# Attention over 8,192 context rows on one core: one PSUM bank moved from scores to maxima, a sixth slot for exponentials, and three steps moved

## The chip, the cores and the metric

The kernel runs on one core of one Trainium2 chip. The metric is the device time of one execution in microseconds (us), as the median of several runs. The engines are called PE (TensorE), DVE (VectorE), ACT (ScalarE), POOL (GpSimd) and SP (SyncE, which only issues transfers here).

## The reference, cut to what matters

Two batches of 512 tokens (x, 512 wide) go through three residual blocks: attention to a context of 8,192 rows of 384 numbers, then a Mamba-like block with an MLP, then a quantised feed-forward block. The change touches the first of them, and the edges of the second by the PSUM banks:

```
x = x + xattn(layernorm(x), ctx_768, ...)
x = x + attn(layernorm(x), ...)
x = x + ffn(layernorm(x), ...)

def xattn(x, y, ...):                       # 16 heads of 32
    q = (x @ Wq + bq); k = (y @ Wk + bk); v = (y @ Wv + bv)
    scores = einsum('bnhd,bmhd->bhnm', q, k) / sqrt(32)
    out = einsum('bhnm,bmhd->bnhd', softmax(scores), v)
    return relu(out @ W1 + b1) @ W2 + b2
```

## The kernel before, in words

**Tiling.** The context is worked in 16 chunks of 1,024 rows (8 for each batch). A chunk has four groups of four heads, so there are 64 groups. I call a chunk's groups first to fourth. A group has 32 units: 8 tiles of 128 context rows by 4 heads. `UPG` is 32, `NGT` is 64, `HG` is 4, `MT` is 8. I number the scores of a group 0 to 31. The loop's step i of line 1942 issues score i + 2, so the code's "step 16 of a group" is where score 18 is issued, step 24 belongs to score 26, and step 29 to score 31.

**Two passes over the keys.** The softmax is done in running form. A first pass (`fill("A")`, line 1828) multiplies queries by keys into a work bank, and DVE takes the maximum of each 128x512 tile (`empty`, line 1052). When a group's 32 maxima are there, `new_max` (lines 1078 and 1080) forms the new running maximum `mn` and its negative `nm`; PE transposes it (line 1832, the item "M"), DVE splits it into `Th` and `Tl`, and SP writes it as extra rows beside the queries. The second pass (`scores`, line 1854) multiplies again, with the maxima subtracted, into one of the score banks; ACT takes the exponential of each 128x512 score into `pf` (`probabilities`, line 1536). The first pass runs 41 units ahead: just before score 23 of a group stands the first fill of the group after next, which waits for that group's keys (`keys_stacked`, line 1826).

**Keys and values.** `fill_side` (lines 1805 and 1812) computes them in pieces between the scores, from the context as two rounded parts, `cTh` (rounded, ACT, line 1493) and `cTl` (the remainder, POOL, line 863). Keys come in halves K0 and K1, values as V0 and V1, all in bank 7. The second half of the keys, K1, is begun just behind score 3. When it is done, ACT and DVE copy it out (KH, KL), and SP issues twelve transfers that stack it into `ks` (`stack_keys`, line 656).

**Weighted values and sums.** Every eighth step PE multiplies two tiles of `pf` by the values (`burst`, `values`, line 1867, rows `x16` in the trace). `pf` has `P_SLOTS` = 5 slots of one tile (4 heads) each. For the denominators POOL adds the tiles 0 to 6 of a group into `psum` (six additions of 128x2048, line 899); tile 7 is added by an accumulating transfer that POOL issues (line 905). Then PE sums over the partitions (`sums`, line 1884) at burst `SUM_BURST`. A slot is free for ACT when PE has used it and POOL has added it; for tile 7's slot that means when the transfer has landed. With five slots this wait stands ahead of the exponential of score 16 of the next group.

**POOL's other duties in a group:** after the third addition `keep_max` (line 873), which waits for DVE's `mn`; behind the transfer `rescale` (line 855); and in the second group of a chunk both halves of the next chunk's `cTl`, the first half ahead of the first addition, the second ahead of the sixth (`LOW_AT`). ACT computes the scaling factor `al` of the next group (`shrink`, line 1507) at step 24.

**PSUM.** Eight banks of 128x512: work banks 0 and 1 (`WORK_BANKS`; maxima and the transposes M, T and D take turns there), score banks 2, 3 and 4, the denominators in 5, the outputs in 6, keys and values in 7. A fill waits until DVE has emptied the tile `WORK_BANKS` before it; a score waits for the exponential `S_BANKS` before it:

```
pe.wait_ge(s_wfree, work_count(x))            # fill, line 1819
if u >= S_BANKS:                              # scores, line 1850
    pe.wait_ge(s_exp, (u - S_BANKS + 1))
```

**The lead-in** (lines 1919 to 1941) turns the normalised x of both batches, computes q in banks 2 to 5, and the first keys, values and maxima. All order is written out by hand in each engine's block.

Of the kernel before, what the change touches and what calls it, by code (L numbers as in the profile page):

```python
# [30 lines left out]
MT = CH // P  # L31
# [28 lines left out]
NGT = NB * NGB  # L60
UPG = HG * MT
UNITS = NGT * UPG
A_UNITS = NT * BLK
A_AHEAD = UPG + 9
WORK_BANKS = 2
S_BANK = 2
S_BANKS = 3
DEN_BANK = 5
O_BANK = 6
SIDE_BANK = 7  # L70
# [19 lines left out]


LOW_GROUP = 1
LOW_AT = {0: 0, 5: 1}
P_SLOTS = 5
BURST = 2
BURSTS = NGT * MT // BURST
ADDS = MT - 2
KEEP_ADD = 3
LAST_SUMMED = 4
LAST_ADDS = LAST_SUMMED - 1  # L100
SUM_BURST = MT // BURST + 1
STEPS = (NGT - 1) * UPG + T_LAG + D_LAG + 1
ATTENDED = UNITS - UPG + T_LAG - UPG + 2
TURNED = UNITS + BURST * HG + 2
# [30 lines left out]
def work_at(i):  # L135

    u, items = i + SB_AHEAD, []
    if u + A_AHEAD < NGT * HG * A_UNITS:
        items.append(("A", u + A_AHEAD))
    if u % UPG == M_STEP and u // UPG + 1 < NGT:  # L140
        items.append(("M", u // UPG + 1))
    g, r = divmod(i - T_LAG, UPG)
    if 0 <= g < NGT and r == 0:
        items.append(("T", g))
    if 0 <= g < NGT and r == D_LAG and g % NG == NG - 1:
        items.append(("D", g // NG))
    return items
# [16 lines left out]
def high_at(i):  # L164

    u = i + SB_AHEAD
    c, half = u // (NG * UPG) + 1, HIGH_AT.get(u % (NG * UPG))
    return [(c, half, f) for f in range(KC)] if half is not None and c < NB * NCH else []


def low_at(g, n):

    c = g // NG + 1
    if g % NG == LOW_GROUP and n in LOW_AT and c < NB * NCH:
        return c, LOW_AT[n]
    return None
# [4 lines left out]
WORK_POS, SIDE_POS = {}, {}  # L181
# [3 lines left out]
    if _x not in SIDE_POS:  # L185
        SIDE_POS[_x] = len(SIDE_POS)
WORK_N, SIDE_N = len(WORK_POS), len(SIDE_POS)
assert WORK_N % WORK_BANKS == 0


def side_bank(x):
# [5 lines left out]
def side_ends(i):  # L197

    part = side_at(i)
    return part[0] if part and last_piece(*part) else None  # L200
# [44 lines left out]
def stage(b, name):  # L245

    n = {"ln_q_T": NT, "q": KD, "att_T": NT, "xw1": F1 // P, "xw2": NT, "rms_T": NT, "xz": 2 * KD, "dbc": 1,
         "dt": KD, "conv": KD, "ssm": KD, "mix_out": NT, "ln2_T": NT, "ffn1": F2 // P, "ffn2": NT, "ln3_T": NT, "lora1": 1,
         "fc": F2 // P, "lora2": 1, "proj": NT}[name]
    return [(b, name, i) for i in range(n)]  # L250
# [2 lines left out]
ALL_BANKS = tuple(range(8))  # L253
LOW, HIGH = ALL_BANKS[:4], ALL_BANKS[4:]
SEGMENTS = [
    ((2, 3, 4, 5), stage(0, "ln_q_T") + stage(0, "q") + stage(1, "ln_q_T") + stage(1, "q")),
    ((7, 2, 3, 4), stage(0, "att_T") + stage(0, "xw1")),
    (ALL_BANKS, stage(1, "att_T") + stage(0, "xw2")
     + stage(1, "xw1")[:AHEAD_1] + stage(0, "rms_T") + stage(0, "xz")[:6] + stage(0, "dbc") + stage(0, "dt")
     + stage(0, "xz")[6:] + stage(1, "xw1")[AHEAD_1:]),  # L260
# [21 lines left out]
def emit(nc, t_in, out):  # L282
    with ExitStack() as ctx:
# [3 lines left out]
        def sb(name, shape, dt=F32, c=ctx):  # L287
            return c.enter_context(nc.sbuf_tensor(name, shape, dt))
# [96 lines left out]
        ps = ctx.enter_context(nc.psum_tensor("ps", [P, 8, 512], F32))  # L385
# [59 lines left out]

        pf = sb("pf", [P, P_SLOTS, HG * NTOK], c=att)
        psum = sb("psum", [P, 2, HG * NTOK], c=att)
# [11 lines left out]
        def place(name, at, shape, dt=F32):  # L459

            with ExitStack() as c:
                if at:
                    sb("below_" + name, [P, at], mybir.dt.uint8, c)
                return sb(name, shape, dt, c)
# [19 lines left out]
        xw1 = place("xw1", 96 * K, [P, 2, KD, F1 // 2])  # L484
# [95 lines left out]
        def work_count(x):  # L580

            return WORK_POS[x] + 1

        def work_bank(x):

            return ps[:, WORK_POS[x] % WORK_BANKS, :]

        def side_count(x):

# [20 lines left out]
        def _(sp):  # L610
# [33 lines left out]
            def save_out(b):  # L644

                sp.wait_ge(s_wfree, work_count(("D", b * NCH + NCH - 1)) + WORK_BANKS)
                sp.dma_start(o_rows[b], Oacc[:]).then_inc(s_osave, 16)
# [11 lines left out]
            def max_rows(g):  # L659

                sp.wait_ge(s_wfree, work_count(("M", g)) + WORK_BANKS)
                for r, src in enumerate((Th, Tl)):
# [168 lines left out]
        def _(pool):  # L831
# [15 lines left out]
            def rescale(of):  # L847

                pool.wait_ge(s_alpha, of + 1)
                if of >= NG:  # L850
                    pool.wait_ge(s_wfree, work_count(("D", of // NG - 1)) + WORK_BANKS)
                if of // NG == NCH:
# [35 lines left out]
            for g in range(NGT):  # L888
# [4 lines left out]
                for n in range(adds):  # L893
# [3 lines left out]
                    pool.wait_ge(s_exp, HG * (tile + 1))  # L897
                    before = pf[:, (tile - 1) % P_SLOTS, :] if n == 0 else acc
                    pool.tensor_tensor(acc, before, pf[:, tile % P_SLOTS, :], ALU.add).then_inc(s_sum, 1)  # L899
                    pool.wait_ge(s_sum, g * ADDS + (n + 1))  # L900
                    if n == KEEP_ADD - 1 and g + 1 < NGT:
                        keep_max(g + 1)
                if g < NGT - 1:
                    pool.wait_ge(s_exp, HG * (g + 1) * MT)
                    pool.dma_start(acc, pf[:, (g * MT + MT - 1) % P_SLOTS, :], accum_op=ALU.add
                                   ).then_inc(s_tail, 16)
# [11 lines left out]
        def _(dve):  # L918

            dve.memset(cols[:, COL["eps"][0]:COL["eps"][0] + 1], EPS).then_inc(s_eps, 1)  # L920
            for i in range(8):
                dve.memset(stats[0][:, 0, 0:1], 0.0).then_inc(s_free[i], 1)
                dve.wait_ge(s_free[i], 1)
            dve.memset(stats[0][:, 0, 0:1], 0.0).then_inc(s_wfree, WORK_BANKS)
            dve.wait_ge(s_wfree, WORK_BANKS)
# [546 lines left out]
        def _(act):  # L1472
# [16 lines left out]
            def high_context(c, i, f):  # L1489

                part = slice(i * CH // 2, (i + 1) * CH // 2)
                act.wait_ge(s_ctx[i], 16 * (c + 1))
                act.copy(cTh[:, f, part], cT[:, f, part]).then_inc(s_chi[i], 1)
# [8 lines left out]
            def shrink(of):  # L1502

                act.wait_ge(s_dm, of + 1)
                if of > 1:
                    act.wait_ge(s_resc, of - 1)
                act.activation(al[:, of % 2, :], dm[:], ACT.Exp, scale=SCALE).then_inc(s_alpha, 1)

            def take_side(x):

                act.wait_ge(s_side, side_count(x))
                src = ps[:, side_bank(x), :]
                if x[0] == "K":
                    if x[1] > 0:
                        keys_stacked(act, x[1] - 1)
                    act.activation(KH[:, x[2] * 512:(x[2] + 1) * 512], src, ACT.Identity,
                                   bias=col("bk", x[1] % NG)).then_inc(s_kvh, 1)
                else:
                    pair, q = x[1] // 2, x[1] % 2 * 2 + x[2]
                    if q == 0 and pair >= 2:  # L1520
                        act.wait_ge(s_pv, MT * (2 * pair - 2))
                    act.copy(V[:, pair % 2, q * VM:(q + 1) * VM, :].rearrange("p m d -> p (m d)"), src  # L1522
                             ).then_inc(s_vfree, 1)

            def probabilities(u):

                act.wait_ge(s_sb, (u + 1))
                tile, j = divmod(u, HG)
                if j == 0 and tile >= P_SLOTS:
                    of, r = divmod(tile - P_SLOTS, MT)  # L1530
                    act.wait_ge(s_pv, of * MT + (r + 1))
                    if r < MT - 1:
                        act.wait_ge(s_sum, of * ADDS + max(r, 1))
                    else:
                        act.wait_ge(s_tail, 16 * (of + 1))
                act.activation(pf[:, tile % P_SLOTS, j * NTOK:(j + 1) * NTOK], ps[:, S_BANK + u % S_BANKS, :],  # L1536
                               ACT.Exp, scale=SCALE).then_inc(s_exp, 1)
# [32 lines left out]
            for i in range(STEPS):  # L1570
                side = side_ends(i - 1)
                if side and side[0] == "K":
                    take_side(side)
                if i + SB_AHEAD < UNITS:
                    probabilities(i + SB_AHEAD)
                if side and side[0] == "V":
                    take_side(side)
                for part in high_at(i):
                    high_context(*part)
                if i % UPG == 1 and 1 <= i // UPG <= NGT:  # L1580
                    take_out(i // UPG - 1)
                if i % (NG * UPG) == BURST * HG * (SUM_BURST - MT // BURST + 1) + 1 and i // (NG * UPG) > 0:
                    take_sums(i // (NG * UPG) - 1)
                for x in work_at(i):
                    if x[0] == "M":
                        shrink(x[1])
            arrive(act)

            def hidden(b, fs):
# [135 lines left out]
            for j in range(PAIRS):  # L1725
                b, i = divmod(j, S_ALL)
                q, e = divmod(i, KD)
# [30 lines left out]
        def _(pe):  # L1758
# [84 lines left out]
            def scores(u):  # L1843
# [4 lines left out]
                if n == 0:  # L1848
                    pe.wait_ge(s_mrow[g % NG], (g // NG + 1) * 32)
                if u >= S_BANKS:  # L1850
                    pe.wait_ge(s_exp, (u - S_BANKS + 1))
                if u == UPG * (KS - 1):
                    pe.wait_ge(s_ones2, 16)
                pe.matmul(ps[:, S_BANK + u % S_BANKS, :], ks[0:SROWS, keys_of(g, j), m * P:(m + 1) * P],  # L1854
                          qs[0:SROWS, h, :], start=True, stop=True).then_inc(s_sb, 1)
# [42 lines left out]
            def burst(n):  # L1898

                if n < BURSTS:  # L1900
                    for tile in range(BURST * n, BURST * (n + 1)):
                        values(tile)
                g, rest = divmod(n - SUM_BURST, MT // BURST)
                if g >= 0 and rest == 0:
# [319 lines left out]
```

## Time and profile before

| what | us |
|---|---|
| median of 3 runs | 3052.53 (3051.62 to 3055.20) |
| profiled execution | 3053.57 |
| its span, first to last instruction | 3051.7 |
| busy PE / DVE / POOL / ACT | 2932.7 / 2237.6 / 2021.2 / 1676.0 |
| mean granted TensorE clock | 0.990 |

The lead-in lasts until score 0 at 87.67 us, the loop over groups until about 2260 us, and the rest of the program to the end. Matmuls overlap one another in the trace (a 512-column one shows as 0.40 us, but the next starts 0.23 us later), so the starts are to be read, not the sum of the durations. In a row of the timeline the bracket at the end gives the idle time before the row, and whose work ended it.

### The profile page before, as it was taken

To read this page: it belongs to the slowest core of one execution; us is meant where nothing else is said; L and a number is where in the kernel's file an instruction comes from. 1 tells how busy PE (TensorE), PEld (TensorE's weight loads), DVE (VectorE), ACT (ScalarE), POOL (GpSimd) and SP (SyncE) were. 2 spreads that over 40 slices of the span, in tenths; PEclk is the share of its full clock that TensorE was granted. 3 is DMA by queue.
4 is the path that set the end of the run, shared out by engine and by line. 5 is a ranking of instruction groups with operands and counts; after the bars stand their busy time and mean duration, and the time that the engine had idled before them with its cause. 6 is when DMAs were issued, how large, how long until landed. Compare 5 with 4: busy or idle time off the path is not lost. (4 is left out here: it accounts for less than half of the span.)

```text
span 3051.7 us, 39907 instructions
## 1 busy us (share of the span) xinstructions
PE 2932.7 (96%) x14712; PEld 1802.4 (59%) x14712; DVE 2237.6 (73%) x3368; ACT 1676.0 (55%) x2920; POOL 2021.2 (66%) x745
## 2 busy tenths in 40 slices
PE   7999999999999999999999999999999877899999
PEld 4666666666666666666666666666534333344477
DVE  7777777777777777777777777777746899986653
ACT  1566666666666666666666666666641555321021
POOL 1699998999999998999999899999950000000000
PEclk9999999999999999999999999999999999999999
DMA  6534543454435455453444444443450112214200
GB/s 166 136 81 101 114 107 91 96 116 100 101 84 115 102 122 126 104 121 87 101 95 118 95 95 104 114 104 81 87 178 25 47 63 97 79 59 167 69 14 18
DMA packets 108886, 296.10 MB, mean 97 GB/s; under 512 B 23762, under 2 KB 28882, under 8 KB 99122
## 3 DMA queue, kind: packets, MB, share of 16 engines
q1 hardware_dynamic: 99044, 226.71, 26.8%
q0 software_dynamic: 9072, 66.06, 11.8%
q8 instruction: 117, 1.92, 0.3%
q10 hardware_dynamic: 576, 0.79, 0.1%
q14 instruction: 77, 0.63, 0.1%
HBM read 114.46 MB, written 8.06 MB: 40 GB/s over the span
## 5 line engine op out<-in xcount | busy, mean ns | idle before, releaser
L1052 DVE TENSOR_REDUCE pm<-ps 128x1 f32<-128x512 f32 x2048 | 1407.8, 691 | 542.3 <-PE ps L1828 472.2
L1536 ACT ACTIVATE pf<-ps 128x512 f32<-128x512 f32 x2048 | 1212.4, 599 | 707.9 <-PE ps L1854 562.6
L899 POOL TENSOR_TENSOR psum<-psum,pf 128x2048 f32<-128x2048 f32 x317 | 1455.9, 4593 | 25.1 <-ACT pf L1536 8.9
L1828 PE MATMUL ps<-ks,qs 96*128 96x512 f32 x2048 | 847.5, 414 | 21.0 <-DVE pm L1052 12.5
L1854 PE MATMUL ps<-qs,ks 98*128 98x512 f32 x2048 | 813.8, 398 | 2.3 <-ACT pf L1536 2.2
L1828 PEld LDWEIGHTS ps<-ks,qs 96*128 96x128 f32 x2048 | 387.0, 189 | 284.9 <-issue 155.8
L1867 PE MATMUL ps<-pf,V 128*32 128x512 f32 x4096 | 492.7, 598 | 0.0
L1854 PEld LDWEIGHTS ps<-qs,ks 98*128 98x128 f32 x2048 | 391.0, 191 | 50.1 <-ACT pf L1536 13.8
L914 POOL PARTITION_ALL_REDUCE qstat<-qstat x2 | 0.7, 365 | 603.2 <-DVE qstat L1350 603.2
L899 POOL TENSOR_TENSOR psum<-pf 128x2048 f32<-128x2048 f32 x64 | 303.1, 4735 | 37.0 <-ACT pf L1536 36.9
L1805 PE MATMUL ps<-cTh,Wkg 128*128 128x512 f32 x732 | 293.2, 401 | 13.4 <-POOL cTl L863 10.2
L1867 PEld LDWEIGHTS ps<-pf,V 128*32 128x32 f32 x4096 | 106.7, 109 | 244.0 <-issue 197.8
L1812 PE MATMUL ps<-Wvh,cTh 128*128 128x256 f32 x768 | 224.3, 292 | 0.0
L1812 PE MATMUL ps<-Wvl,cTh 128*128 128x256 f32 x768 | 219.0, 285 | 0.0
L1812 PE MATMUL ps<-Wvh,cTl 128*128 128x256 f32 x768 | 218.0, 284 | 0.0
L2057 PE MATMUL ps<-bx,ident 128*128 128x512 f32 x256 | 134.7, 655 | 54.1 <-DVE bx L1320 54.1
L1805 PEld LDWEIGHTS ps<-cTh,Wkg 128*128 128x128 f32 x732 | 139.0, 190 | 60.8 <-ACT V L1522 30.1
L1812 PEld LDWEIGHTS ps<-Wvl,cTh 128*128 128x128 f32 x768 | 146.5, 191 | 27.2 <-issue 1.5
L1812 PEld LDWEIGHTS ps<-Wvh,cTh 128*128 128x128 f32 x768 | 146.1, 190 | 25.9 <-issue 1.2
L1812 PEld LDWEIGHTS ps<-Wvh,cTl 128*128 128x128 f32 x768 | 145.9, 190 | 22.5 <-issue 1.0
L1314 DVE TENSOR_TENSOR_SCAN bx<-dA,bx 128x512 f32<-128x512 f32 x128 | 149.3, 1208 | 1.5 <-ACT dA L1734 1.4
L1805 PE MATMUL ps<-cTl,Wkg 128*128 128x512 f32 x366 | 144.8, 396 | 0.0
(224 smaller groups left out, 3016.0 us busy)
## 6 DMA issues: line engine op xcount, KB each, us to landing
ks<-KH SPq DMA_DIRECT2D x512, 128.0 KB, 3.5
psum<-pf POOLq DMA_DIRECT2D x63, 1024.0 KB, 8.0
ks<-KL SPq DMA_DIRECT2D x256, 128.0 KB, 3.5
cT<-in_ctxT SPq DMA_DIRECT2D x32, 768.0 KB, 4.7
Wkg<-wk_rows SPq DMA_DIRECT2D x61, 384.0 KB, 5.8
BC<-bc_rows SPq DMA_DIRECT2D x32, 512.0 KB, 4.8
ring<-in_ffn_w SPq DMA_DIRECT2D x16, 1024.0 KB, 7.9
wA<-in_W_fcT SPq DMA_DIRECT2D x4, 1024.0 KB, 10.3
```

The costliest lines, as they stand in the source:

```text
L899: pool.tensor_tensor(acc, before, pf[:, tile % P_SLOTS, :], ALU.add).then_inc(s_sum, 1)
L914: pool.partition_all_reduce(qstat[:, i, 1:2], qstat[:, i, 0:1], P, bass.bass_isa.ReduceOp.max).then_inc(s_allmax, 1)
L1052: dve.tensor_reduce(pm[:, n // BLK, n % BLK:n % BLK + 1], src, AX.X, ALU.max).then_inc(s_wfree, 1)
L1314: last = dve.tensor_tensor_scan(bx[:, slot, s, :], dA[:, slot, s, :], bx[:, slot, s, :], 0.0, ALU.mult, ALU.add)
L1536: act.activation(pf[:, tile % P_SLOTS, j * NTOK:(j + 1) * NTOK], ps[:, S_BANK + u % S_BANKS, :], ACT.Exp, scale=SCALE).then_inc(s_exp, 1)
L1805: last = pe.matmul(dst, w[term == 2], (cTh, cTl)[term == 1][:, f, half], start=(n == 0), stop=(n == TERMS - 1))
L1812: last = pe.matmul(dst[:, m * 2 * P:(m + 1) * 2 * P], (cTh, cTl)[term == 2][:, f, t * P:(t + 1) * P], (Wvh, Wvl)[term == 1][:, f, pair], s ...
L1828: last = pe.matmul(dst, qs[0:3 * HD, h, t * P:(t + 1) * P], ks[0:3 * HD, keys_of(of, j), i * 512:(i + 1) * 512], start=True, stop=True)
L1854: pe.matmul(ps[:, S_BANK + u % S_BANKS, :], ks[0:SROWS, keys_of(g, j), m * P:(m + 1) * P], qs[0:SROWS, h, :], start=True, stop=True).then_ ...
L1867: last = pe.matmul(ps[j * HD:(j + 1) * HD, O_BANK, :], V[:, g // 2 % 2, m, at:at + HD], pf[:, tile % P_SLOTS, j * NTOK:(j + 1) * NTOK], st ...
L2057: last = pe.matmul(bank(w), ident[:], bx[:, j % S_SLOTS, s, :], start=(q == 0 and s == 0), stop=(q == S_PER - 1 and s == S_STEP - 1))
```

## The change: what it does

- Work banks: 0, 1 and 4 (three). Score banks: 2 and 3 (two). Bank 4 is taken out of the turns for the lead-in's transposes and queries (now 2, 3, 5) and for the first transposes and products behind the loop (now 7, 2, 3).
- `P_SLOTS` 6: the wait for the transfer of tile 7 stands ahead of the exponential of score 20.
- `SUM_BURST` one later: the sums are issued at step 24, behind score 26, no longer at step 16, behind score 18. ACT's copy of a chunk's denominators (`take_sums`) moves with it.
- `LOW_AT`: the second half of `cTl` ahead of the fifth addition.
- `SHRINK_STEP`: ACT's `al` at step 29.
- The scratch space in SBUF for the transfers that POOL issues: 512 for 2048.

```diff
-WORK_BANKS = 2
+WORK_AT = (0, 1, 4)
+WORK_BANKS = len(WORK_AT)
 S_BANK = 2
-S_BANKS = 3
+S_BANKS = 2
...
-LOW_AT = {0: 0, 5: 1}
-P_SLOTS = 5
+LOW_AT = {0: 0, 4: 1}
+P_SLOTS = 6
...
-SUM_BURST = MT // BURST + 1
+SUM_BURST = MT // BURST + 2
+SHRINK_STEP = UPG - 3
...
-    ((2, 3, 4, 5), stage(0, "ln_q_T") + stage(0, "q") + stage(1, "ln_q_T") + stage(1, "q")),
-    ((7, 2, 3, 4), stage(0, "att_T") + stage(0, "xw1")),
+    ((2, 3, 5), stage(0, "ln_q_T") + stage(0, "q") + stage(1, "ln_q_T") + stage(1, "q")),
+    ((7, 2, 3), stage(0, "att_T") + stage(0, "xw1")),
...
-            return ps[:, WORK_POS[x] % WORK_BANKS, :]
+            return ps[:, WORK_AT[WORK_POS[x] % WORK_BANKS], :]
...
-                for x in work_at(i):
-                    if x[0] == "M":
-                        shrink(x[1])
+                if i % UPG == SHRINK_STEP and i // UPG + 1 < NGT:
+                    shrink(i // UPG + 1)
...
-    nc = _bacc.Bacc("TRN2", target_bir_lowering=False, num_devices=1, dynamic_dma_scratch_size=2048)
+    nc = _bacc.Bacc("TRN2", target_bir_lowering=False, num_devices=1, dynamic_dma_scratch_size=512)
```

**PE around the sums.** On PE, in every group, before, from the scores 17 and 18 to the next pieces of keys:

```order
L1854 MATMUL ps<-qs,ks 128x512
L1867 MATMUL ps<-pf,V 32x512 x8
L1884 MATMUL ps<-psum,sel 32x512 x4
L1828 MATMUL ps<-ks,qs 128x512
L1854 MATMUL ps<-qs,ks 128x512
L1805 MATMUL ps<-cTh,Wkg 128x512
```

and with the change, in the same group, first the same place and then (behind the line of dots) that of scores 25 to 27:

```order
L1854 MATMUL ps<-qs,ks 128x512
L1867 MATMUL ps<-pf,V 32x512 x8
L1828 MATMUL ps<-ks,qs 128x512
L1854 MATMUL ps<-qs,ks 128x512
L1805 MATMUL ps<-cTh,Wkg 128x512
...
L1832 MATMUL ps<-ident,nm 16x128
L1867 MATMUL ps<-pf,V 32x512 x8
L1884 MATMUL ps<-psum,sel 32x512 x4
L1828 MATMUL ps<-ks,qs 128x512
L1854 MATMUL ps<-qs,ks 128x512
```

The four matmuls of the sums (L1884) leave the place between score 18 and fill and score 19, and stand eight scores later, behind the transposed maxima (L1832) and the next burst.

**POOL in the second group of a chunk,** before, from the copies of `keep_max` to the transfer:

```order
L884 COPY pm<-m_run 128x16
L899 TENSOR_TENSOR psum<-psum,pf 128x2048 x2
L863 TENSOR_TENSOR cTl<-cT,cTh 128x3x512
L899 TENSOR_TENSOR psum<-psum,pf 128x2048
L905 DMA psum<-pf 128x2048
```

and with the change (its lines are one further down):

```order
L885 COPY pm<-m_run 128x16
L900 TENSOR_TENSOR psum<-psum,pf 128x2048
L864 TENSOR_TENSOR cTl<-cT,cTh 128x3x512
L900 TENSOR_TENSOR psum<-psum,pf 128x2048 x2
L906 DMA psum<-pf 128x2048
```

One addition passes behind the remainder; the transfer stays last.

## Rows read from the trace of the kernel before

**Rows 1.** Who waited for whom, 600 to 2300 us: total, times, longest.
```profile
PE ps L1828 <- DVE pm L1052: 8.2, 17, 1.9
PE ps L1805 <- POOL cTl L863: 7.4, 11, 0.7
```
**Rows 2.** Timeline of PE and DVE, second groups: start, duration, engine, line, what.
```profile
695.04 0.50 PE L1828 MATMUL ps<-ks,qs 96*128 96x512 f32 x1 [0.30 <-DVE pm L1052]
...
1240.64 0.50 PE L1828 MATMUL ps<-ks,qs 96*128 96x512 f32 x1 [1.90 <-DVE pm L1052]
...
693.63 0.76 DVE L1080 TENSOR_SCALAR nm<-mn 128x16 f32<-128x16 f32 x1
```
**Rows 3.** Timeline of PE and POOL, K1 in a third and a first group.
```profile
571.52 0.47 PE L1805 MATMUL ps<-cTh,Wkg 128*128 128x512 f32 x1 [0.67 <-POOL cTl L863]
...
775.08 0.40 PE L1854 MATMUL ps<-qs,ks 98*128 98x512 f32 x1
775.57 0.51 PE L1805 MATMUL ps<-cTh,Wkg 128*128 128x512 f32 x1
...
567.91 3.46 POOL L863 TENSOR_TENSOR cTl<-cT,cTh 128x1536 fp32r<-128x1536 f32 x1
```
**Rows 4.** Timeline of PE, same third group: sums, next fill, and the awaited fill.
```profile
587.21 1.04 PE L1884 MATMUL ps<-psum,sel 128*32 128x512 f32 x8
588.18 0.50 PE L1828 MATMUL ps<-ks,qs 96*128 96x512 f32 x1
...
592.92 0.47 PE L1828 MATMUL ps<-ks,qs 96*128 96x512 f32 x1 [1.20 <-issue]
```
**Rows 5.** Timeline of SP and PE: a stack of keys, third group and then first.
```profile
578.32 0.53 SPq L656 DMA_DIRECT2D ks<-KH  x1
...
646.60 0.53 SPq L656 DMA_DIRECT2D ks<-KH  x1
...
654.98 0.59 SPq L656 DMA_DIRECT2D ks<-KH  x1
...
659.63 0.39 PE L1828 MATMUL ps<-ks,qs 96*128 96x512 f32 x1
```
**Rows 6.** Timeline of POOL and ACT around the third group's start.
```profile
576.24 0.88 POOL L905 DMA_DIRECT2D psum<-pf  x1 [0.30 <-DVE pm L1052]
...
560.85 1.67 ACT L1493 CAST cTh<-cT 128x512 fp32r<-128x512 f32 x3
...
586.76 1.57 ACT L1536 ACTIVATE pf<-ps 128x512 f32<-128x512 f32 x3 [3.42 <-DMA psum<-pf]
```
**Rows 7.** The page, DMA issues: KB each, median us to landing.
```profile
ks<-KH SPq DMA_DIRECT2D x512, 128.0 KB, 3.5
psum<-pf POOLq DMA_DIRECT2D x63, 1024.0 KB, 8.0
```
**Rows 8.** Timeline of ACT and PE: exponentials of scores 4 to 6, then score 6.
```profile
743.26 1.75 ACT L1536 ACTIVATE pf<-ps 128x512 f32<-128x512 f32 x3
...
743.98 0.40 PE L1854 MATMUL ps<-qs,ks 98*128 98x512 f32 x1
```
**Rows 9.** Timeline of PE, POOL and DVE, end of the loop over groups.
```profile
2254.97 1.04 PE L1884 MATMUL ps<-psum,sel 128*32 128x512 f32 x8
...
2192.22 0.22 POOL L873 TENSOR_TENSOR dm<-m_run,mn 128x16 f32<-128x16 f32 x1 [2.01 <-issue]
...
2244.02 9.90 POOL L899 TENSOR_TENSOR psum<-psum,pf 128x2048 f32<-128x2048 f32 x2
...
2260.14 2.87 DVE L983 COPY tT<-ps 128x512 f32<-128x512 f32 x4 [1.53 <-PE ps L1768]
```
**Rows 10.** Timeline of PE and DVE in the lead-in.
```profile
18.13 0.77 PE L1805 MATMUL ps<-cTh,Wkh 128*128 128x512 f32 x1 [1.55 <-DVE cTl L1018]
...
78.50 0.49 PE L1828 MATMUL ps<-ks,qs 96*128 96x512 f32 x1 [1.05 <-DVE pm L1052]
...
19.10 2.86 DVE L983 COPY xqT<-ps 128x512 f32<-128x512 f32 x4
```

More of the change, by code:

```diff
@@ L187 @@
 WORK_N, SIDE_N = len(WORK_POS), len(SIDE_POS)
-assert WORK_N % WORK_BANKS == 0
 def side_bank(x):
```

## The prediction

> **What bounds the kernel now.** I read the page first: PE is busy 96% of the span, and its few idle stretches are what a change like this can win. In the waits of PE inside the loop over groups [rows 1] two causes stand out, 17 waits for DVE's maxima and 11 for POOL's remainder `cTl`. As a matmul shows as 0.40 us but the next starts 0.23 us later, a matmul with idle time g before it is late by g + 0.17. So [rows 1] come to 8.2 + 17 x 0.17 = 11.1 us and 7.4 + 11 x 0.17 = 9.3 us in 1,660 us. Next I placed each wait in its group by the timeline, and it is always the same three places in a chunk of four groups (some 136 us):
>
> - Second group, fill before score 25: late by 0.47 us, once by 2.07 [rows 2]. DVE has just reduced the last maximum of a group and formed `mn` and `nm`, and with two work banks PE can't run ahead of it. Sixteen groups have it, 12 of them inside [rows 1] with 7.3 us of the 11.1; all sixteen come to 9.8 us.
> - Third group, first key matmul of K1: late by 0.84 us, since the second half of `cTl` ends at 571.4 [rows 3]. Fifteen groups.
> - Third group, fill before score 23: late by 1.37 us in this chunk [rows 4]. Its releaser is shown as "issue", once and again as DVE; what it really waits for are the twelve transfers of the new keys. In this third group the fill starts 592.92 - 578.32 = 14.60 us after the first of them was issued; in a first group 659.63 - 646.60 = 13.03 us, without idle, and there the last transfer was issued at 654.98, so that it landed before 659.63 by the page's 3.5 us [rows 5, 7]. In the third group POOL's 1 MB transfer was issued at 576.24, 2.1 us before the keys' first [rows 6], and both share the DMA engines. I looked at all fifteen: 13.6 to 14.8 us, mean 14.1.
>
> ACT waits too, 3.42 us for the landing of POOL's transfer ahead of the exponential of score 16 [rows 6]. In PE that is only a late copy of V0 behind score 18, 0 to 0.6 us, which in turn shortens the wait before score 23: the keys decide.
>
> **The change part by part.**
>
> 1. *Third work bank.* The fill before score 25 now needs the maximum three before it. DVE needs 0.69 us for one and a step of PE is 0.70 us, so the bank forgives 0.7 us: the usual 0.47 goes, of the 2.07 some 1.4 stays, of one of 1.12 another 0.4. Each late matmul also costs 0.1 us behind it. 9.8 + 1.6 - 1.8 - 0.2: **-9.4 us**. Bounds: 0 (if DVE is late for another reason each time) and -11.4.
>
> 2. *Second half of `cTl` one addition earlier.* It would end 4.6 us sooner, at 566.8. Its input `cTh` is written by ACT until 562.5 [rows 6], 0.6 us before the fourth addition ends, so POOL doesn't wait. Then K1 waits for the copy of V0, as it does in a first group: 775.57 - 775.08 - 0.23 = 0.26 us [rows 3]. Gain 0.84 - 0.26 = 0.58, 15 times: **-8.7 us**. Bounds: 0 and -12.6.
>
> 3. *Sums behind score 26.* They take 588.18 - 587.21 = 0.97 us of PE [rows 4], of which I take 0.9 (a burst straight before a fill has a tail too). PE's total is the same, but they leave the stretch between the keys' first transfer and the fill before score 23. Where that stretch is set by the transfers, PE now waits 0.9 us longer, and the sums come on top behind it. Fifteen third groups: **+13.5 us**. In the other groups PE needs 13.03 - 0.9 = 12.1 us there and the keys were in time by 0.7 to 3.3 us; only the tightest is then late: **+0.3 us**. Bounds: 0 (the keys land sooner by as much) and +14.6. Waits of the sums for the transfer, 0.04 to 0.5 us in some third groups, are already inside.
>
> 4. *Sixth slot.* ACT's wait moves to score 20. In third groups the transfer landed 2.8 us ahead of score 20; the sums' move and items 1 and 2 take 2 us of that, so ACT hardly waits. The copy of V0 is in time, but its gain goes into the wait before score 23: **0**. If that cover were gone, it would be -2.7 us.
>
> 5. *Two score banks.* A score now waits for the exponential two before it. The tightest place is score 6: in [rows 8] three exponentials run from 743.26 in 1.75 us, so the first (score 4) ends at 743.86, and score 6 starts at 743.98: 0.12 us of room, where 0.06 is needed. Other steps have 0.37 or more; the only negative ones stand behind ACT's wait for the transfer, which item 4 takes away. **0**. Bounds: nothing, and one late ACT copy (0.58 us, 0.26 more than the 0.37 of room less 0.06) in each of 62 groups, +16.
>
> 6. *`al` at step 29.* 0.24 us of ACT beside steps with 0.5 us of room: **0**. The smaller scratch: POOL's issue takes 0.88 us [rows 6] and a transfer is over before the next is issued, 34 us later: **0**.
>
> 7. *End of the loop.* The last sums wait for POOL, whose chain has no gap from its last wait for DVE at 2192.2 (2.01 us long) to the end of its additions at 2253.92 [rows 9]. DVE's `mn` there comes 0.9 us sooner, as the sums have moved behind it, so POOL ends at 2253.0, and the sums can start there rather than at 2254.97, because ACT is no longer held up from score 16 on. The transposes and DVE's copies, at 2260.14, follow: **-1.8 us**. The three banks for them cost nothing: the fourth transpose waits for a copy of 0.7 us that DVE makes anyway.
>
> 8. *Lead-in.* The fourth transpose of x now waits for DVE's first copy, which ends at 19.8; before, the keys could start at 18.13 [rows 10]. They start at about 20.8, run through both halves, and the second half, bound by DVE's `cTl` before, ends 1.3 us later: +1.3. The maxima's waits (1.22 us at 78.50 [rows 10], 0.7 behind it, a few of 0.1 to 0.4) shrink: -2.3. **-1.0 us**; bounds +2.3 and -2.3.
>
> Sum: -9.4 - 8.7 + 13.5 + 0.3 - 1.8 - 1.0 = **-7.1 us** against the profiled execution's own 3053.6, so 3046.5; the median of the runs lies 1.0 below that one, so **3045.5 us**.
>
> **A rule against a row.** POOL's 1 MB transfers take 8.0 us in the median [rows 7], and item 3 rests on that: the transfer is under way for most of the keys' stack. The Trainium skill ("DMA: Bandwidth & Descriptors", Anatomy of one DMA — SWDGE (gpsimd) path) fits such a transfer as 2.0 us plus its bytes over 436 GB/s, an estimate of 4.4 us here, over soon after the keys begin. By it the keys would land as in other groups and rival A holds; this trace disagrees (7.0 at least).
>
> **Rivals.**
>
> - *A: the keys aren't the gate, or land sooner.* Then item 3 costs nothing and item 4 gains: 3045.5 - 13.5 - 2.7 = 3029. For it: the trace names DVE for some of these waits. Against: third groups take 13.6 us or more each time, with or without the late V0.
> - *B, the other side: two score banks.* If any of ACT's copies runs one place later than now, PE waits at once: at score 6, or where the room is 0.37. Price +16 (item 5): 3062. It decides from 0.06 us at score 6. Against: ACT's order hardly moves.
> - *C: the gains come short.* `nm` took 0.76 us in [rows 2] while POOL was adding. An addition takes 4.6 us; if `nm` meets it earlier, DVE is late by more than a bank forgives, and item 1 shrinks to -3; with a lead-in at +2.3: 3045.5 + 6.4 + 3.3 = 3055. The Trainium skill ("SBUF — State Buffer", Who interferes with whom) has it as a lock held for a whole instruction, which the 2.07 us fits. Against: in second groups DVE and POOL both move by 0.9 us, so they meet as before.
> - *D: the smaller scratch* makes POOL wait for its own transfer: some 7 us a group on an engine with about 1.6 us to spare, +300 us. Nothing in the trace speaks for it.
>
> **How the numbers follow.** Forecast 0.50, A 0.14, B 0.11, C 0.24, D 0.01. A measurement tells about 0.2%, 6.1 us. The forecast's own spread is 4 us around 3045.5, so six in ten of it lie below 3046.4: faster 0.31 + 0.14 = 0.45 and a little of C, 0.46. Slower (above 3058.6): B, D and a little of C, 0.13. The same: 0.41. The range takes in A's and C's values and half of what leads to B: 3028 to 3058. Both signs are likely, so the forecast's own range: 3041 to 3050.
>
> **What would show it.** Right: no wait before score 25 in second groups; K1's start in third groups 0.26 us late, by V0; in third groups the fill before score 23 still 14 us behind the keys' first transfer, and PE's wait there about 2.0 us instead of 1.0; sums without waits; end of the loop near 2253. Wrong: that wait unchanged or gone (A), scores that wait for exponentials (B), `nm` above 1.5 us or fills that still wait (C).

## The result, and the profile after

The changed kernel takes 3067.16 us (median of 6 runs, 3063.45 to 3079.47) against 3053.32 us before (6 runs, 3051.62 to 3055.20): ratio 1.0055, 95% interval [1.0043, 1.0068]. The forecast was 3045.5 with a range from 3028 to 3058. The kernel became slower by 0.55%, beyond the noise, and the prediction was wrong in sign.

| what | before | after |
|---|---|---|
| profiled execution | 3053.57 | 3068.36 |
| score 32 starts (lead-in over) | 123.94 | 125.17 |
| score 32 to score 1984 | 2075.85 | 2078.22 |
| score 1984 to 2047 (last two groups) | 52.82 | 64.20 |
| from there to the end | 801.0 | 800.8 |
| mean granted TensorE clock | 0.990 | 0.984 |

The starts are those of the rows of L1854. Of the 14.8 us between the two executions 11.4 lie in the last two groups, 2.4 in the 61 before them, 1.2 in the lead-in, and the rest is 0.2 shorter.

**The waits of PE in the loop,** after, 600 to 2300 us (waited for, total, times, longest), answer to [rows 1]:

```profile
PE ps L1828 <- issue: 17.4, 11, 2.2
PE ps L1854 <- ACT pf L1537: 4.6, 16, 0.5
PE ps L1828 <- DVE pm L1053: 1.6, 2, 0.9
PE ps L1832 <- DVE nm L1081: 1.1, 1, 1.1
```

The 17 waits for DVE have become 2, the 11 for `cTl` are gone. Two kinds have grown. The 11 waits of 17.4 us are those of the awaited fill of third groups, where the same 11 groups had 6.3 us before. The 16 waits of scores for exponentials (5 before, 1.4 us) all stand behind 2209 us, in the last two groups: up to 2200 us neither profile shows one.

**A second group,** after, timeline of POOL, DVE and PE around score 25 [rows 2]. `nm` takes 0.76 us as before, and the fills at 694.83 and 695.53 have no idle time before them:

```profile
690.73 4.60 POOL L900 TENSOR_TENSOR psum<-psum,pf 128x2048 f32<-128x2048 f32 x1
...
694.60 0.76 DVE L1081 TENSOR_SCALAR nm<-mn 128x16 f32<-128x16 f32 x1
694.60 0.40 PE L1805 MATMUL ps<-cTh,Wkg 128*128 128x512 f32 x1
...
694.83 0.40 PE L1828 MATMUL ps<-ks,qs 96*128 96x512 f32 x1
695.07 0.40 PE L1854 MATMUL ps<-qs,ks 98*128 98x512 f32 x1
...
695.53 0.40 PE L1828 MATMUL ps<-ks,qs 96*128 96x512 f32 x1
```

**The third group of rows 3 to 6,** after, timeline of PE, POOL and SP:

```profile
563.06 3.51 POOL L864 TENSOR_TENSOR cTl<-cT,cTh 128x1536 fp32r<-128x1536 f32 x1
...
570.50 0.40 PE L1854 MATMUL ps<-qs,ks 98*128 98x512 f32 x1
...
570.99 0.50 PE L1805 MATMUL ps<-cTh,Wkg 128*128 128x512 f32 x1
...
576.17 0.90 POOL L906 DMA_DIRECT2D psum<-pf  x1 [0.37 <-DVE pm L1053]
...
577.80 0.53 SPq L657 DMA_DIRECT2D ks<-KH  x1
...
589.63 0.59 SPq L657 DMA_DIRECT2D ks<-KH  x1
...
592.12 0.48 PE L1828 MATMUL ps<-ks,qs 96*128 96x512 f32 x1 [1.99 <-issue]
592.43 0.50 PE L1854 MATMUL ps<-qs,ks 98*128 98x512 f32 x1
...
593.16 0.63 PE L1828 MATMUL ps<-ks,qs 96*128 96x512 f32 x1
593.58 0.63 PE L1854 MATMUL ps<-qs,ks 98*128 98x512 f32 x1
```

K1 is late by 0.26 us, as forecast. But POOL issues its transfer at 576.17, where before it was 576.24 [rows 6]. The group starts at the same time as before (566.29 and 566.25) and PE has gained some 1.6 us in it, 0.6 at K1 and 1.0 by the moved sums; half of that shows in the fill, which comes at 592.12 for 592.92, and half has become wait, 1.99 us for 1.20. The fill does wait for the keys: by the trace's landing times the last of the twelve, issued at 589.63, lands at 592.03, and the fill starts 0.09 us later. The same 0.09 us stands behind each of the 94 such fills with idle time above 0.2 us in the seven kernels below where they wait. POOL's transfer has landed by then, at 585.66. Behind the fill the matmuls stand 0.42 us apart and show as 0.63: the granted clock has fallen from 2.4 to 1.2 GHz. Two such stretches, windows of after (PE, PEld, DVE, ACT, POOL busy, then the granted clock, DMA share, GB/s):

```profile
592.20:596.00 3.80, 3.80 (x10) 2.96 (x11) 2.08 (x3) 1.66 (x3) 3.74 (x4) 0.55 0.00 0
...
1278.30:1282.30 4.00, 3.96 (x11) 3.12 (x12) 2.19 (x4) 1.63 (x3) 3.86 (x5) 0.57 0.01 2
```

A fall lasts 3.41 us here; there are five in the loop, all straight behind this fill where it was 1.87 to 2.41 us late. Before there was none, and this fill was late by 1.54 us at most.

**The last two groups,** windows of before and then of after, the same columns:

```profile
2215.00:2230.00 15.00, 14.52 (x83) 5.44 (x80) 5.64 (x11) 9.40 (x19) 14.70 (x6) 1.00 0.26 89
2230.00:2245.00 15.00, 11.64 (x68) 4.24 (x60) 4.91 (x4) 7.50 (x15) 14.54 (x6) 1.00 0.92 284
```

```profile
2215.00:2230.00 15.00, 13.54 (x66) 5.55 (x68) 10.65 (x17) 8.52 (x16) 14.70 (x6) 0.92 0.14 28
2230.00:2245.00 15.00, 13.11 (x44) 3.90 (x36) 0.00 (x0) 8.59 (x17) 13.46 (x6) 0.73 0.90 317
2245.00:2260.00 15.00, 13.40 (x53) 4.63 (x53) 6.76 (x5) 9.20 (x17) 13.74 (x4) 0.84 0.26 53
```

PE does 44 instructions where it did 68, at a granted clock of 0.73 where it had 1.00. The timeline there, of before and then of after:

```profile
2225.57 4.03 ACT L1536 ACTIVATE pf<-ps 128x512 f32<-128x512 f32 x8 [1.53 <-PE ps L1854]
2226.22 2.46 PE L1854 MATMUL ps<-qs,ks 98*128 98x512 f32 x5 [0.22 <-ACT pf L1536]
2228.61 1.92 PE L1867 MATMUL ps<-pf,V 128*32 128x512 f32 x16
2230.47 0.96 PE L1854 MATMUL ps<-qs,ks 98*128 98x512 f32 x3
2231.00 0.60 ACT L1536 ACTIVATE pf<-ps 128x512 f32<-128x512 f32 x1 [1.40 <-PE ps L1854]
```

```profile
2217.40 9.20 POOL L900 TENSOR_TENSOR psum<-psum,pf 128x2048 f32<-128x2048 f32 x2
...
2223.56 0.98 PE L1854 MATMUL ps<-qs,ks 98*128 98x512 f32 x2 [0.21 <-ACT pf L1537]
...
2224.24 2.40 DVE L1081 TENSOR_SCALAR nm<-mn 128x16 f32<-128x16 f32 x1
...
2226.78 0.27 PE L1832 MATMUL ps<-ident,nm 128*16 128x128 f32 x1 [1.05 <-DVE nm L1081]
...
2226.98 3.13 PE L1867 MATMUL ps<-pf,V 128*32 128x512 f32 x16
...
2229.86 1.60 PE L1884 MATMUL ps<-psum,sel 128*32 128x512 f32 x8
2231.39 0.73 PE L1854 MATMUL ps<-qs,ks 98*128 98x512 f32 x2
2231.92 2.97 ACT L1537 ACTIVATE pf<-ps 128x512 f32<-128x512 f32 x5 [5.56 <-PE ps L1854]
```

Behind the last fill PE has only scores, values, sums and a few transposes. Scores go two at a time where they went three to five at a time, a burst takes 3.13 us at the lower clock for 1.92, and ACT, with at most two scores in stock, stands idle for 5.56 us beside late `nm`, the burst and the sums.

### The profile page after: what moved, and what is told of

The parts are those of the page before. It is cut to its first block, busy times and chain, and to the rows that moved or that the text cites. A ratio compares the mean times of both kernels' runs of the same rounds, so it can differ in the third digit from the quotient of the medians.

```text
span 3066.6 us, 39906 instructions
## 1 busy us (share of the span) xinstructions
PE 2946.3 (96%) x14712; PEld 1814.0 (59%) x14712; DVE 2250.4 (73%) x3368; ACT 1685.1 (55%) x2920; POOL 2022.5 (66%) x745
## 3 DMA queue, kind: packets, MB, share of 16 engines
q8 instruction: 117, 1.92, 0.3%
## 4 chain that ended last, share of the span: by engine, by line
PE 89%; DVE 7%; ACT 2%; issue 2%; DMA 0%; SPq 0%; ACTq 0%; DVEq 0%
PE ps L1828 16%; PE ps L1867 16%; PE ps L1854 15%; PE ps L1781 9%; PE ps L1812 9%; PE ps L1805 8%; PE ps L2077 4%; PE ps L2041 4%; PE ps L2057 2%; PE ps L1884 2%; DVE pm L1053 2%; DVE bx L1315 1%; PE ps L1836 1%; PE ps L2069 1%; ACT V L1523 1%
## 5 line engine op out<-in xcount | busy, mean ns | idle before, releaser
L1854 PE MATMUL ps<-qs,ks 98*128 98x512 f32 x2048 | 824.0, 403 | 6.8 <-ACT pf L1537 6.5
L1854 PEld LDWEIGHTS ps<-qs,ks 98*128 98x128 f32 x2048 | 393.1, 192 | 75.9 <-ACT pf L1537 31.9
```

## The experiments

Three theories were put up after this reading. Theory 1, mine: the moved sums lengthen the wait of third groups, and the clock falls behind it. Theory 2: all of the loss is the two score banks. Theory 3: the sums' move costs nothing. Theory 4 came out of the first four runs.

**Undoing parts.** sums_back:

```diff
-SUM_BURST = MT // BURST + 2
+SUM_BURST = MT // BURST + 1
```

> The changed kernel with the sums at step 16 again, behind score 18; all else as changed. Theory 1 (the moved sums make PE wait 1.9 us and more ahead of score 23 in some third groups, the granted clock falls to 0.5 for 3.4 us after it, and the two score banks cost only at the end of the loop): that wait goes back to about 1.0 us, no fall of the clock between 101 and 2200 us, 3.4 us less by score 1984 for each of the chunks at 137.7 us or more (five, some 9 us) and 13 us for the waits themselves: 3067 - 22 = 3045 us, the last two groups still some 10 us too long. Theory 2 (all of the loss is in the two score banks): the waits go, but only by what they are, 13 us: 3054 us or more, and the chunks keep falls of the clock. Theory 3 (moving the sums costs nothing, the keys land with them): 3065 to 3069.

Measured 3062.33 us (ratio 1.0041 [1.0029, 1.0053]): 5 us better by the medians, 3.4 us against the kernel before beside each, and not 22. The intervals of the two ratios overlap, and the loop of the profile is no shorter (2079.05 us, 2078.22 with the sums moved). The third groups are as long (the table below), and the clock still falls. So the sums don't carry the loss as theory 1 had it, and theory 3's figure was nearest.

banks_back undoes the banks:

```diff
-WORK_AT = (0, 1, 4)
+WORK_AT = (0, 1)
...
-S_BANKS = 2
+S_BANKS = 3
...
-    ((2, 3, 5), stage(0, "ln_q_T")
+    ((2, 3, 4, 5), stage(0, "ln_q_T")
...
-    ((7, 2, 3), stage(0, "att_T")
+    ((7, 2, 3, 4), stage(0, "att_T")
```

> The changed kernel with two work banks and three score banks again, and the lead-in and the first stages behind the loop on their old banks; all else as changed. Theory 1: the 10 us of groups 62 and 63 and some 2 us ahead of score 6 come back, the fills ahead of score 25 are late again (9.4 us), and the falls of the clock in third groups stay: 3067 - 12 - 1 + 9 = 3063. Theory 2 (the score banks are all of the loss, 24 us against the forecast): 3067 - 24 + 9 = 3052. In both, score 2047 stands less than 26 us behind score 2016 (before 25.3, changed 33.3).

Measured 3048.61 us (0.9990 [0.9982, 0.9999]), better than either theory had it, and less than before, with the sums moved. So the banks carry the whole loss and more; the 51.8 us of the last two groups bear out that part.

sums_banks_back is both edits together; low_only is the kernel before with `LOW_AT = {0: 0, 4: 1}`.

> The changed kernel with both taken back: what is left is the sixth slot, the second half of cTl ahead of the fifth addition, al at step 29 and the small scratch. Theory 1: the forecast's item 2 alone, -8.7 us, and up to -2.7 more where the copy of V0 is no longer held up: 3042 to 3045 us, and no fall of the clock in the loop. A rival (the small scratch or the sixth slot costs something of its own): above 3048.

> The kernel before with only the second half of cTl ahead of the fifth addition. By item 2 of the prediction -8.7 us: 3044.5 us, K1 in third groups late by 0.26 us. If instead the gain only goes into the wait ahead of score 23, which the keys' landing sets after K1's own start: since the keys are issued sooner by as much, it should not; a result above 3049 would speak for that.

Measured 3047.68 us (0.9983 [0.9974, 0.9992]) and 3047.95 us (0.9988 [0.9979, 0.9996]). The sixth slot, the small scratch and `al` together cost and bring nothing in the medians (0.8 us in the loops of the profiles). Between these runs the sums' move costs 0.9 us (3048.61 against 3047.68; 3.1 us in the loop of the profiles, 2068.53 and 2071.66), where the forecast had 13.8. With three work banks the median shows 4.8 (sums_back), without a trace of it in the loop.

**What gates the third group.** The table puts the profiles side by side: mean time from score 0 of second and third groups to the next group's, then in third groups the issue of POOL's transfer and the awaited fill, both behind score 0, and the time at half clock and for the last two groups (starts of rows; the means are over 15 groups).

| kernel | 2nd group | 3rd group | transfer | fill | half clock, loop | last two groups |
|---|---|---|---|---|---|---|
| before | 34.28 | 35.23 | 10.02 | 26.18 | 0 | 52.8 |
| low_only | 34.37 | 34.58 | 9.99 | 25.50 | 3.4 | 53.6 |
| sums_banks_back | 34.53 | 34.47 | 9.94 | 25.30 | 6.8 | 54.9 |
| banks_back | 34.66 | 34.56 | 9.05 | 24.59 | 6.8 | 51.8 |
| after | 33.79 | 35.87 | 9.88 | 25.43 | 17.1 | 64.2 |
| sums_back | 33.69 | 35.99 | 10.70 | 26.72 | 10.2 | 64.3 |
| short_add | 33.80 | 33.54 | 5.60 | 23.69 | 0 | 61.7 |
| tile7_pe | 33.80 | 34.40 | none | 24.55 | 0 | 62.4 |
| late_banks | 33.80 | 36.29 | 9.89 | 25.56 | 27.3 | 54.5 |
| tile7_late | 33.80 | 34.40 | none | 24.55 | 0 | 53.5 |
| tile7_banks_back | 34.77 | 34.38 | none | 24.54 | 10.2 | 52.5 |
| tile7_late_sums_back | 33.69 | 34.39 | none | 25.41 | 0 | 55.1 |

In the seven kernels where the fill waits, it stands in the mean 15.4 to 16.2 us behind POOL's issue, but 13.1 to 15.2 us behind the first issue of the keys. Moving the sums makes POOL's issue come 0.9 us sooner behind score 0 (9.94 to 9.05), and the third work bank makes it come 0.8 us later (9.05 to 9.88), since the second group is shorter and POOL's chain is not: counted from score 0 of the second group (the first two columns added, second group and transfer) POOL's issue comes at 43.71 us in banks_back and 43.67 in after. The awaited fill, counted so, comes at 59.25 and 59.22: what the bank gains in the second group, 0.87 us, is gone at that fill. In banks_back no third group has a fall of the clock behind it (its 6.8 us stand in second groups), with fills late by 1.43 us at most.

That is theory 4: POOL's transfer and the keys share the DMA engines (from 576 to 593 us in after the keys' queue takes 49.2% of the 16 engines and POOL's 31.1%), and the pair is over a fixed time behind POOL's issue. The fixed time is one of means; single fills stand 14.7 to 17.3 us behind POOL's issue, and what sets the rest isn't shown. Two runs change the transfer itself, one by leaving it out, one by issuing it sooner. tile7_pe (`tail_by_pe(g)` is true for second groups, and the second piece stands in `values`; the changed waits of ACT and of the sums are left out here):

```diff
-                    pool.wait_ge(s_exp, HG * (g + 1) * MT)
-                    pool.dma_start(acc, pf[:, (g * MT + MT - 1) % P_SLOTS, :], accum_op=ALU.add
-                                   ).then_inc(s_tail, 16)
+                    if not tail_by_pe(g):
+                        pool.wait_ge(s_exp, HG * (g + 1) * MT)
+                        pool.dma_start(acc, pf[:, (g * MT + MT - 1) % P_SLOTS, :], accum_op=ALU.add
+                                       ).then_inc(s_tail, 16)
...
+                if m == MT - 1 and tail_by_pe(g):
+                    for j in range(HG):
+                        pe.matmul(ps[j * HD:(j + 1) * HD, DEN_BANK, :], sel[:, g % NG, :],
+                                  pf[:, tile % P_SLOTS, j * NTOK:(j + 1) * NTOK], start=False, stop=False)
```

> The changed kernel, but in second groups POOL issues no transfer: tile 7 of the group is summed by PE, four matmuls ahead of its values. Theory 4 (formed from the first four runs: in every group of every kernel the keys land 15.2 to 16.5 us behind the issue of POOL's transfer, so in third groups it is POOL's transfer, issued 9.9 us behind score 0, that sets the fill ahead of score 23, not the issue of the keys): without it the keys land in time as far as 12 us behind their issue suffice; the wait of 1.7 us and the falls of the clock behind it (0.4 us a group in the mean) go, PE pays 0.9 us for the four matmuls: 15 x (0.9 - 2.2) = -20 us: 3047 us. Theory 1 (the keys take 13.8 us from their own issue on): the wait stays, and with the four matmuls at most 0.9 us of it are covered: 3067 or more.

Measured 3041.54 us (0.9963 [0.9950, 0.9975]), some 5 us under theory 4's figure.

short_add leaves most of one tile out of the denominators of each second group, so its result is not the reference's and its time serves only to test the theory:

```diff
+                    cut = slice(0, 64 if g % NG == LOW_GROUP and n == ADDS - 1 else HG * NTOK)
-                    pool.tensor_tensor(acc, before, pf[:, tile % P_SLOTS, :], ALU.add).then_inc(s_sum, 1)
+                    pool.tensor_tensor(acc[:, cut], before[:, cut], pf[:, tile % P_SLOTS, cut], ALU.add).then_inc(s_sum, 1)
```

> The changed kernel, but POOL's sixth addition of each second group takes in only 64 of 2048 columns: most of that tile is left out of the sums, and POOL issues the transfer 4.5 us sooner. Theory 4: the keys land with it, the wait ahead of score 23 in third groups goes, and the clock's falls: 3067 - 33 = 3034 us. Theory 1: 3065 us, the wait unchanged.

Measured 3028.02 us (0.9919 [0.9906, 0.9932]). Its timeline in the same group, SP and PE:

```profile
564.03 0.89 POOL L907 DMA_DIRECT2D psum<-pf  x1 [0.37 <-POOL psum L901]
...
569.97 0.52 SPq L657 DMA_DIRECT2D ks<-KH  x1
...
577.20 1.32 SPq L657 DMA_DIRECT2D ks<-KH  x1
...
582.14 0.40 PE L1829 MATMUL ps<-ks,qs 96*128 96x512 f32 x1
```

The fill is 12.17 us behind the keys' first transfer and doesn't wait; SP issues the twelve in 8.5 us (569.97 to 578.52), where beside the late transfer it needed 12.4 (577.80 to 590.22 in after's timeline, its last issue at 589.63 lasting 0.59). In both runs no third group waits, and the clock doesn't fall once between score 32 and score 1984. Theory 1's gate, the keys' own 13.8 us, has fallen: it asked for 3067 or more and for 3065 us. In the kernels without the transfer in second groups the keys of third groups land 9.8 to 9.9 us behind their first issue in the mean, and beside it 13.0 to 15.0 us: so POOL's transfer is what makes them late.

**The end of the loop.** late_banks gives bank 4 back to the scores behind the last fill (the changed waits that go with it are left out here):

```diff
+LATE_U = UNITS - A_AHEAD + 1
+LATE_W = WORK_POS[("A", UNITS - 1)] // len(WORK_AT) * len(WORK_AT)
+def score_bank(u):
+    return S_BANK + (u % S_BANKS if u < LATE_U else (2, 0, 1)[(u - LATE_U) % 3])
...
-            return ps[:, WORK_AT[WORK_POS[x] % WORK_BANKS], :]
+            n = WORK_POS[x]
+            return ps[:, WORK_AT[n % WORK_BANKS if n < LATE_W else (n - LATE_W) % 2], :]
```

> The changed kernel with bank 4 given back to the scores from score 24 of group 62 on, behind the last fill: three score banks and two work banks from there. If the 11 to 12 us lost in groups 62 and 63 are the two score banks: from score 1984 to score 2047 52 to 54 us in place of 64, and 3055 us. If they are DVE's late nm in group 62 (2.4 us) with the clock's falls behind it: 60 us or more, and above 3062.

Measured 3060.51 us (1.0024 [1.0013, 1.0035]; 3049.10 to 3067.16 in 12 runs). The last two groups take 54.5 us for 64.2, as the first reading had it: the two score banks, and not `nm`, which takes 2.33 us there still. Its timeline there:

```profile
2236.65 0.97 PE L1864 MATMUL ps<-qs,ks 98*128 98x512 f32 x3
2237.19 2.56 ACT L1545 ACTIVATE pf<-ps 128x512 f32<-128x512 f32 x5 [5.79 <-PE ps L1864]
2237.84 2.46 PE L1864 MATMUL ps<-qs,ks 98*128 98x512 f32 x5 [0.22 <-ACT pf L1545]
...
2240.23 1.92 PE L1877 MATMUL ps<-pf,V 128*32 128x512 f32 x16
```

Runs of three to five scores are back, and the burst behind them takes 1.92 us. The median came 5 us short of its forecast; the profiled execution of this kernel had 27.3 us at half clock in the loop, ten more than after's, and was itself one of the slowest of the twelve (3066.55).

**A better version, and the parts in it.** tile7_late is tile7_pe and late_banks together; tile7_banks_back is tile7_pe on the old banks; tile7_late_sums_back is tile7_late with the sums at step 16.

> Both of these edits. Theory 4 and the score banks at the end: 3067 - 20 - 12 = 3035 us, which would beat the kernel before by 0.5%. Theory 1: 3055 us.

> The kernel without the transfer in second groups, but with two work banks and three score banks as before. What the third work bank is worth once POOL's transfer no longer gates the third group. Theory 4 (two gates one behind the other: with the transfer in place what the bank gains in the second group is lost again in the third): the waits ahead of score 25 in second groups stay (0.75 us, 15 times), those of third groups are gone, and the end of the loop is as before: 3037 + 11 - 2 (score 6) = 3046 us. If the bank is worth nothing even then: 3037 us or less.

> The best kernel so far (no transfer in second groups, bank 4 given back at the end) with the sums at step 16 again. Theory 4: with no transfer in the third group the place of the sums doesn't matter there; in the other groups the keys are in time with either (1.6 to 2.4 us of room): 3037 us, within 3. If the sums' place has a cost of its own: the kernel differs by 5 us or more.

Measured 3037.31 us (0.9947 [0.9936, 0.9959]), 3047.28 us (0.9985 [0.9976, 0.9994]) and 3033.03 us (0.9936 [0.9923, 0.9949]). The third work bank, worth less than nothing in the change, is worth 10 us once POOL's transfer doesn't gate the third group (3047.28 to 3037.31, and 14.3 us between score 32 and 1984 of the profiles, where tile7_banks_back has 10.2 us at half clock and the other none). The last is the fastest that computes the whole reference, 18.5 us below the 3051.56 of before beside it. The old place of the sums is 4.3 us better there by the medians, 3.2 against the kernel before beside each, where I had given 3 for the same; 1.6 us of it show in the loop of the profiles, the rest I can't place.

## Why the prediction was wrong, point by point

**Which steps failed.** In the profiles the sum was -7.1 us and became +14.8. Two terms made the kernel slower. Item 5 put the two score banks at 0; in the last two groups, where no fill stands between the scores, they cost some 10 us of the +11.4 that stand where item 7 had -1.8. Item 1 priced the third work bank at -9.4; in the loop it cost 6.6, because what it gained came back as a wait on the awaited fill. These errors are of 13 and 16 us. Item 3, with +13.8 for 3.1 in the loop, erred by 10.7 us the other way and hid part of them, which was luck. The same step failed in items 1 and 3: the landing of the keys was counted from their own first issue, with POOL's transfer as a fixed part of it.

- **Item 1, third bank, -9.4.** Right as far as the second group goes: it went from 34.66 to 33.79 us between banks_back and after, 0.87 us in the mean. The sum over the loop was wrong. The next gate, POOL's transfer, hangs on POOL's chain, and that doesn't shorten with PE's second group: third groups went from 34.56 to 35.87, 0.83 us by the transfer's later issue, the rest mostly by the clock. From score 32 to 1984 the bank costs 6.6 us (2071.66 to 2078.22), though the awaited fill comes no later: some 2 us are score 6, and 17.1 us at half clock for 6.8 make an estimate of 5 us, half of the difference. Rival C's sign did appear: `nm` takes 1.4 to 2.0 us in the fifteen third groups of after. But it begins while PE waits for the keys, and from 600 to 2200 us PE shows no wait for `nm`; in second groups it was long twice, 2.22 and 3.24 us.
- **Item 2, `cTl`, -8.7.** Right in the loop: 8.1 us in the loop of low_only (2075.85 to 2067.77); its median shows 4.0 of them, ratio 0.9988.
- **Item 3, sums, +13.5 and +0.3.** "What it really waits for are the twelve transfers of the new keys" was right: the fill starts 0.09 us behind the last landing. Wrong was what sets that landing, 14 us counted from the keys' own issue. The row of the shared engines was cited beside it [rows 6], but taken as a fixed part of the keys' time, and not as what moves. The mean from POOL's issue is as constant, and the move of the sums pulls that issue forward by 0.9 us. It costs 0.9 us in the medians, 3.1 in the loop. Rival A had "or land sooner", and with it the side on which this item erred, but not what lands them sooner. The Trainium skill's fit of such a transfer ("DMA: Bandwidth & Descriptors", Anatomy of one DMA — SWDGE (gpsimd) path), an estimate of 4.4 us here, is as far off as before: the profile of after has 7.8 us in the median.
- **Items 4 and 6, 0.** Right together: sums_banks_back against low_only, 3047.68 and 3047.95; so rival D is out.
- **Item 5, two score banks, 0.** Wrong twice. Score 6 of second and fourth groups is late by 0.07 us, some 2 us in all, where I had seen 0.12 us of room and a need of 0.06. And the check of the steps ended where fills end: the last 41 scores have no fill between them. Rival B had the side and the part of the machine right, and the place wrong.
- **Item 7, end of the loop, -1.8.** It became +11.4, some 10 of it from the cause just named (9.7 came back in late_banks). I had followed POOL and DVE there, and never asked what paces PE when it has only scores.
- **Item 8, lead-in, -1.0.** It was +1.2, but the seven profiles with this same lead-in have score 32 between 122.00 and 125.17: no verdict.
- **The clock** had no term. A PE wait was priced by its length; behind the longest ones in third groups come 3.41 us at 1.2 GHz. At scores 23 to 25 of third groups this makes 0.42 us in the mean of after, some 6 us in all, and in the last two groups 20.5 us stand at that clock.

How the 10 us of the end divide between waits and clock isn't settled: four profiles with two score banks there have 61.7 to 64.3 us with 20.5 to 23.9 us at half clock, eight with three banks 51.8 to 55.1 us with 0 to 6.8. No run has the one without the other. `nm`'s 2.40 us in group 62, which is rival C's sign in another place, wasn't tried by itself, but late_banks keeps 2.33 of it and has 54.5 us.

## What to carry to other kernels

When a wait ends on a transfer that shares the DMA engines with another, count its time from the issue of each of them, and see in other groups and kernels which count stays nearer to constant, then test it by moving or leaving out one of them; after that ask which engine's chain sets the issue, because a gain on another engine can come back as a longer wait. A buffer that is traded away is to be checked where the work beside it ends, not only in the steady loop. And a wait on PE costs more than its length where the granted clock falls behind it, so a change that gathers small waits into a long one can lose by that alone.

## What the runs showed of the hardware

- Twelve key transfers of 128 KB took SP 8.5 us to issue in a third group of short_add and 12.4 us beside POOL's accumulating transfer of 1 MB in the same group of after. That one took 9.7 us from issue to landing in third groups and 7.7 in the others (means of after).
- The fill that waited for the keys started 0.09 us behind the landing of the last one, 94 times of 94.
- The stretches at 1.2 GHz from score 32 to the last score lasted 3.41, 6.83 or, in sums_back, short_add and tile7_pe, once 13.65 us. In after's third groups five fills late by 1.87 to 2.41 us had one behind them; one late by 1.91 us had none, nor had before's fill at 1240.64, late by 2.07 us [rows 2]. So the length of the wait alone doesn't decide it.
- `nm`, 128x16 on DVE, took 0.76 us in one group, 2.40 in another and 3.24 in a third (at 1240.76 in after), each time until 0.02 to 0.04 us behind the end of POOL's addition beside it (690.73 + 4.60, 2217.40 + 9.20, 1234.74 + 9.24).
